# The second graph-attention layer swept head pair by head pair instead of row block by row block

## The reference

```python
xt = jnp.einsum('ni,hio->hno', x, W)              # x: output of layer 0, 4096 x 256
src = jnp.einsum('hnf,hf->hn', xt, a[:, :out_f])
dst = jnp.einsum('hnf,hf->hn', xt, a[:, out_f:])
e = jax.nn.leaky_relu(src[:, :, None] + dst[:, None, :], 0.2)
e = jnp.where(adj > 0, e, -jnp.inf)
h_prime = jnp.einsum('hij,hjf->hif', jax.nn.softmax(e, axis=2), xt)
out = layernorm(x + h_prime.transpose(1, 0, 2).reshape(n, 256))
```

## Time and profile before

| | us |
|---|---|
| median of 3 runs | 2619.55 |
| the profiled execution's own time | 2621.43 |
| its span in the trace | 2619.7 |
| start of the second layer's first group (span time) | 2120.48 |
| start of group 1 | 2157.76 |
| start of its last group | 2581.84 |

### The profile page before, as it was taken

The page is one execution under the profiler, slowest core; times in us unless marked ns, Lnnn a source line. Parts: engine busy times, 40 slices in busy tenths (PEclk is TensorE's granted clock), DMA queues, the critical chain, the costliest instruction groups (busy, mean ns, idle before and its releaser), DMA issues.

```text
span 2619.7 us, 62505 instructions
## 1 busy us (share of the span) xinstructions
PE 2579.8 (98%) x25977; PEld 2300.7 (88%) x25977; DVE 2116.3 (81%) x4315; ACT 2121.9 (81%) x3309; POOL 107.0 (4%) x151
## 2 busy tenths in 40 slices
PE   8999999999999999999999999999999989999998
PEld 6678888888888888888888888888888879999998
DVE  5568888888888888877878778788755689999998
ACT  4578888888888888888888888888873578999997
POOL 1220000000000000000000000000002420000000
PEclk9999999999999999999999999999999999999999
DMA  8975424243342433421212111221226665233430
GB/s 275 321 239 131 111 81 118 63 115 98 90 120 68 124 87 84 110 73 48 64 40 54 50 47 44 60 56 35 62 55 198 228 216 189 95 119 105 132 126 20
DMA packets 324116, 285.02 MB, mean 109 GB/s; under 512 B 124661, under 2 KB 268024, under 8 KB 323834
## 3 DMA queue, kind: packets, MB, share of 16 engines
q1 hardware_dynamic: 290570, 264.51, 34.3%
q10 hardware_dynamic: 33264, 16.52, 2.1%
HBM read 195.13 MB, written 57.74 MB: 97 GB/s over the span
## 4 chain that ended last, share of the span: by engine, by line
PE 88%; DVE 6%; ACT 4%; issue 1%; DMA 0%; SPq 0%; DVEq 0%; ACTq 0%
PE l_ps L912 69%; PE l_ps L1002 8%; PE l_ps L884 4%; PE l_ps L932 4%; ACT l_arena L1238 4%; DVE l_arena L1724 2%; DVE l_arena L1723 2%; PE l_ps L951 1%; DVE l_arena L1749 1%; DVE l_arena L1747 0%; PE l_ps L896 0%; DVE l_arena L1782 0%; DVE l_arena L1712 0%; PE l_ps L857 0%; PE l_ps L943 0%
## 5 line engine op out<-in xcount | busy, mean ns | idle before, releaser
L912 PE MATMUL l_ps<-l_arena 128*128 128x258 f16 x16384 | 1802.4, 273 | 0.6 <-ACT l_arena L1112 0.6
L912 PEld LDWEIGHTS l_ps<-l_arena 128*128 128x128 fp8e4 x16384 | 1603.0, 98 | 200.3 <-ACT l_arena L1112 1.2
L1134 ACT ACTIVATE l_arena<-l_arena 128x512 fp8e4<-128x512 f32 x2048 | 1282.1, 709 | 78.2 <-PE l_ps L912 76.4
L1523 DVE SCALAR_TENSOR_TENSOR l_arena<-l_arena,l_mask 128x512 uint32<-128x512 uint32 x512 | 354.0, 691 | 201.6 <-ACT l_arena L1134 199.3
L1002 PE MATMUL l_ps<-l_arena 128*128 128x130 f16 x8000 | 462.8, 221 | 19.1 <-DVE l_arena L1749 15.1
L1238 ACT ACTIVATE l_arena<-l_arena 128x1024 fp8e4<-128x1024 f32 x434 | 457.6, 1136 | 28.5 <-PE l_ps L1002 28.5
L1002 PEld LDWEIGHTS l_ps<-l_arena 128*128 128x128 fp8e4 x8000 | 459.8, 99 | 22.0 <-issue 19.6
L1524 DVE TENSOR_TENSOR l_arena<-l_arena,l_mask 128x512 uint32<-128x512 uint32 x512 | 354.6, 693 | 0.0
L1503 DVE SCALAR_TENSOR_TENSOR l_arena<-l_arena 128x129 f16<-128x129 f32 x960 | 274.4, 349 | 8.4
L1169 ACT COPY l_arena<-l_ps 128x258 f32<-128x258 f32 x256 | 94.6, 369 | 218.9 <-PE l_ps L912 218.9
L1529 DVE SCALAR_TENSOR_TENSOR l_arena<-l_ps,l_arena 128x258 f32<-128x258 f32 x256 | 116.7, 482 | 115.6 <-ACT l_arena L1169 115.6
(11 more groups left out here) (170 smaller groups left out, 1175.3 us busy)
## 6 DMA issues: line engine op xcount, KB each, us to landing
l_arena<-in_adj SPq DMA_DIRECT2D x58, 1024.0 KB, 6.3
l_arena<-uv SPq DMA_DIRECT2D x125, 272.0 KB, 4.8
l_arena<-l_wh SPq DMA_DIRECT2D x120, 256.0 KB, 4.8
l_arena<-l_srow SPq DMA_DIRECT2D x64, 256.0 KB, 3.3
l_arena<-feat SPq DMA_DIRECT2D x32, 512.0 KB, 3.7
feat<-l_arena ACTq DMA_DIRECT2D x63, 256.0 KB, 2.3
l_wh<-l_arena SPq DMA_DIRECT2D x64, 192.0 KB, 6.9
uv<-l_arena SPq DMA_DIRECT2D x8, 1088.0 KB, 5.7
```

Of the source, the lines that this page charges most:

```text
L912: last = nc.tensor.matmul(sums(t, m), pattern(k, m).bitcast(F8)[:, j, t * P:(t + 1) * P], uv[:, slot(v, order[k]) + j, m * WH:m * WH + 2 * ...
L1134: ins = act.activation(pattern(k, 0).bitcast(F8)[:, j, :], s1b[q][:, :], ACT.Relu, bias=kc[:, h, jt:jt + 1], scale=STEEP, saturate=False)
L1523: dve.scalar_tensor_tensor(c, v, ONE8X4, m, ALU.bitwise_xor, ALU.bitwise_and)
```

## The change

The order of the groups becomes two passes: groups 0 to 7 are heads 0 and 1 over blocks 0 to 3, groups 8 to 15 heads 2 and 3 over the same blocks. Both slots keep their head for a whole pass, so `uv2` is loaded once a pass. The first correction of heads 0 and 1 stays where it was. That of heads 2 and 3 is done in groups 2 to 5 in turns 1, 3 and 5, on one chunk at a time in a small buffer, `visitor`: load, multiply, store, wait, load the next. In pass 1 the residual rows are the 128 left columns in `zh`, which SyncE stores back to `x1` and loads again in every second group; in pass 2 the whole rows are in `z` as before, and head 2 is parked in every block. The statistics and the application move to groups 10 to 15, so that block 2's application and the load of block 3's rows fall into the last group.

```diff
-        G2, FIRST, WHOLE = H2 * NB2, H2, CPB - 2
+        G2, PASS, WHOLE = H2 * NB2, 2 * NB2, CPB - 2
+        visitor = at(88768, F16, 2, JC2, W4)
+        zh = at(76416, F32, 4, TPB2, 2 * D2)
...
+        def head2(g):
+            return g // PASS * 2 + g % 2
+
+        def block2(g):
+            return g % PASS // 2
...
-            def store_back(h, c):
-                cols = slice(c * JC2 * W4, (c + 1) * JC2 * W4)
-                sp.wait_ge(s_res, rescaled(h, c))
-                sp.dma_start(uvd[h][:, cols], uv2[:, h % 2, cols]).then_inc(s_back[h], 16)
+            def far_columns(i):
+                c = i % WHOLE
+                return uvd[2 + i // WHOLE][:, c * JC2 * W4:(c + 1) * JC2 * W4]
+
+            def load_far(i):
+                sp.dma_start(visitor.rearrange("p t w -> p (t w)"), far_columns(i)).then_inc(s_in, 16)
+
+            def store_far(i):
+                sp.wait_ge(s_res, 2 * WHOLE + i + 1)
+                sp.dma_start(far_columns(i), visitor.rearrange("p t w -> p (t w)")).then_inc(s_back, 16)
...
+            def load_half(b):
+                sp.dma_start(zh, half_rows(b)).then_inc(s_zl, 16)
+
+            def store_half(b):
+                sp.wait_ge(s_dz, 2 * b + 2)
+                sp.dma_start(half_rows(b), zh).then_inc(s_xs[b], 16)
...
             for g in range(G2):
-                if g > H2 and g % H2 == 1:
-                    b = g // H2 - 1
+                if g in range(2, PASS + 1, 2):
+                    b = g // 2 - 1
+                    store_half(b)
+                    sp.wait_ge(s_xs[b], 16 * (NT // 4 + 1))
+                    if g < PASS:
+                        load_half(b + 1)
+                    else:
+                        for first, last in parts2:
+                            load_z(0, first, last)
+                if g > PASS + 2 and g % 2 == 1:
+                    b = block2(g) - 1
                     for p, (first, last) in enumerate(parts2):
                         sp.wait_ge(s_ap, 3 * b + p + 1)
                         sp.dma_start(tiles(out, b, first, last), z[:, first:last, :]).then_inc(s_o[p], 16)
...
+                if g == 1:
+                    load_far(0)
+                if 2 <= g < 6:
+                    for i in range(3 * (g - 2), 3 * (g - 1)):
+                        store_far(i)
+                        sp.wait_ge(s_back, 16 * (i + 1))
+                        if i + 1 < 2 * WHOLE:
+                            load_far(i + 1)
                 if g < G2 - 2:
                     sp.wait_ge(s_ca2, CPB * (g + 1))
                     sp.wait_ge(s_cd, owned(g, own[-1]))
                     load_row2(g + 2)
-                    if g < FIRST:
-                        sp.wait_ge(s_back[g], 16 * WHOLE)
+                if PASS - 2 <= g < PASS:
                     for k in range(CPB):
                         sp.wait_ge(s_pe2, CPB * g + k + 1)
                         load_uv(g + 2, k)
-                    if g + 1 < FIRST:
-                        for n in range(WHOLE):
-                            store_back(g + 1, n if g % 2 else WHOLE - 1 - n)
...
+            def add_parked(b):
+                dve.wait_ge(s_zl, 16 * NB2 + 48 * (b + 1))
+                dve.tensor_tensor(z[:, :, 2 * D2:3 * D2], z[:, :, 2 * D2:3 * D2], park, ALU.add)
+
+            def rescale_far(i):
+                h, c = 2 + i // WHOLE, i % WHOLE
+                dve.wait_ge(s_in, 16 * (i + 1))
...
-                    if 0 < g < FIRST - 1 and m >= 6:
-                        for n in range(2 * (m - 6), 2 * (m - 5)):
-                            rescale(g + 1, n)
-                    if g >= H2:
-                        b = g // H2 - 1
-                        if g % H2 == 0 and 1 <= m < 5:
+                    if 2 <= g < 6 and m in (1, 3, 5):
+                        rescale_far(3 * (g - 2) + m // 2)
+                    if g > PASS + 1:
+                        b = block2(g) - 1
+                        if g % 2 == 0 and 1 <= m < 5:
                             final_stats(2 * (m - 1), 2 * m, g)
...
-                if 0 < g < FIRST - 1:
-                    for n in range(4, WHOLE):
-                        rescale(g + 1, n)
             base = 2 * NT + 4 * (NB2 - 1)
+            add_parked(NB2 - 1)
```

More of the change, by code:

```diff
@@ L285, in network @@
         s_us, s_res = s.sem("us"), s.sem("res")
-        s_back = [s.sem(f"back{h}") for h in range(H2)]
+        s_in, s_back = s.sem("in"), s.sem("back")
         s_uv2 = [[s.sem(f"uv{q}{k}") for k in range(CPB)] for q in range(2)]
@@ L791, in _ @@
             sp.wait_ge(s_xp, NT)
-            for first, last in parts2:
-                load_z(0, first, last)
+            load_half(0)
             store_rows(CPB - 2)
-            for c in range(WHOLE):
-                store_back(0, c)
             store_rows(CPB - 1)
@@ L981, in sweep2 @@
                     pe.wait_ge(s_bc2, CPB * g + k + 1)
-                    if g < FIRST and order[k] < WHOLE:
+                    if g < 2 and order[k] < WHOLE:
                         pe.wait_ge(s_res, rescaled(g, order[k]))
                     else:
-                        pe.wait_ge(s_uv2[q][k], 16 * (g // 2 + 1))
+                        pe.wait_ge(s_uv2[q][k], 16 * (g // PASS + 1))
                     for t in range(TPB2):
@@ L1746, in drain2 @@
                     ch = Chain(dve, s_e2, 2 * g + t // batch)
[L1747 removed]
+                    ch.link(dve.tensor_tensor(into, sums2(slice(t, t + batch), 1), sc2[:, head2(g), rows:rows + batch].unsqueeze(
                         2).to_broadcast([P, batch, 2 * V1]), ALU.mult))
@@ L1766, in divide2 @@
                 v = part[:, :, 0:D2]
-                quotient = park if h == 0 and b > 0 else v
+                quotient = park if h == 2 else v
                 ch.link(dve.tensor_tensor(quotient, v, inverse.unsqueeze(2).to_broadcast([P, last - first, D2]), ALU.mult))
-                if h == 0 and b > 0:
+                if h == 2:
                     dve.sem_inc(s_dz, 1)
                     return
-                if h == (b > 0):
-                    dve.wait_ge(s_zl, 48 * (b + 1))
-                if h == 1 and b > 0:
-                    dve.tensor_tensor(z[:, :, 0:D2], z[:, :, 0:D2], park, ALU.add)
-                into = z[:, first:last, h * D2:(h + 1) * D2]
-                dve.tensor_tensor(into, into, v, ALU.add).then_inc(s_dz, 1)
+                if h == 0:
+                    dve.wait_ge(s_zl, 16 * (b + 1))
+                elif h == 3:
+                    add_parked(b)
+                into = (zh if h < 2 else z)[:, first:last, h * D2:(h + 1) * D2]
+                dve.tensor_tensor(into, into, v, ALU.add).then_inc(s_dz, 1)
+            def add_parked(b):
[4 more added lines that the diff above has]
+                dve.wait_ge(s_in, 16 * (i + 1))
+                dve.tensor_scalar(visitor[:, :, 0:2 * V1], visitor[:, :, 0:2 * V1], fu.bitcast(F32)[:, c, h:h + 1], None,
+                                  ALU.mult)
+                dve.tensor_scalar(visitor[:, :, VH:VH + 2 * V1], visitor[:, :, VH:VH + 2 * V1],
+                                  fv.bitcast(F32)[:, c, h:h + 1], None, ALU.mult).then_inc(s_res, 1)
             def final_stats(first, last, ready):
```

31 lines of the change are left out of this document (16 added, 15 removed).

## The result

| | median of the runs, us | lowest to highest |
|---|---|---|
| before, on the same chip | 2618.66 (20 runs) | 2612.35 to 2622.27 |
| changed | 2622.89 (20 runs) | 2616.79 to 2627.18 |

The ratio is 1.0017, 95% interval 1.0011 to 1.0023, that is +4.4 us (2.9 to 6.0). The direction was forecast wrong; the time lies inside the range of 2613.5 to 2626.

What follows compares the result with a forecast made beforehand. The prediction took a loop through ScalarE, VectorE and TensorE to set the steady 29.74 us group, leaving gains only in groups 1 to 3. Terms of -4.88, 0, 0 and +3.4 gave -1.5 us: 2618.0 us, range 2613.5 to 2626.

Steps and rivals of the forecast that it cites:

- What bounds the kernel: Second layer: steady groups, 29.74 us, offer nothing; a group starts at earliest 11.40 us after the comparison; gains only in groups 1 to 3.
- Term 1: Groups 1 to 3: corrections of heads 2 and 3 leave, gaining 1.20, 2.05 and 1.63 us (the last from the clock), 4.88 together.
- Term 2: Groups 2 to 5: visiting chunks cost nothing, as a 4.8 us round trip fits VectorE's 5.2 us of other work.
- rival A: Groups 2 to 5: visitors don't keep up and VectorE waits; 5.2 us at a 6.5 us round trip, time 2623.2; chance 0.16.
- Term 3: Division and statistics: three blocks' statistics still cost 0.12 us each and only move to groups 10, 12, 14; nothing.
- Term 4: Last group: late load of residual rows delays the tail's first reading to +26.35 us, a loss of 3.4 us.
- The sum: Whole kernel: -4.88 + 3.4 = -1.5 us, put on the median 2619.55, gives 2618.0 us.
- C: Last group: the tail is cheaper because the load lands sooner; -3.1 us, time 2616.5; chance 0.09.
- D: Start of the layer, groups 0 and 1, runs better without slot traffic; -6 us, time 2613.6; chance 0.08.
- B: Groups 1 to 3: gain doesn't come, as the slow clock turns up elsewhere; +1.4 us, time 2621; chance 0.12.

Runs made afterwards that it cites:

- e2: The kernel before without the corrections of heads 2 and 3 and their stores back (computation left out); ratio 0.9980, -5.2 us.
- e8: The kernel before, its group order kept, with the corrections of heads 2 and 3 moved to earlier turns, none at a group's end; 2614.58 us, ratio 0.9982.
- e9: No computation, only a 272 KB chunk stored and loaded back 96 times with nothing else on the core; 458.9 us, 4.78 a round trip.
- e4: The changed kernel with two visitor buffers instead of one, loads two corrections ahead; ratio 1.0000 against before.
- e5: The changed kernel, unchanged, timed and traced a second time; ratio 1.0025 against before.
- e7: The changed kernel with two visitor buffers, block 2's early application in the last group, and the parked addition moved from VectorE to GpSimd; ratio 0.9996.
- e6: The changed kernel with block 2's application wholly in turn 1 of the last group, so the last load goes out sooner; ratio 1.0015.
- e1: The kernel before, unchanged, timed and traced a second time; ratio 1.0004 against itself.
- e11: No computation, the 96 store-and-load round trips beside busy VectorE and ScalarE only; 457.4 us, run once.
- e3: The changed kernel with head 3's visiting chunks corrected ahead of head 2's; 2618.43 us, one run.

## Why the prediction was wrong, by its own steps

**What bounds the kernel: right.** Steady groups stayed at 29.74, and 11.40 us from the comparison on was indeed the earliest start: e2 and e8 reach it in groups 2 and 3 and nothing goes below.

**Term 1 (-4.88): right.** e2 -5.2, e8 -4.7. All three parts are there in the traces, group 3's clock too. Group 1 of the changed kernel shows 31.37 at a mean clock of 0.95; that slow start was there before and is no gain or loss of the change.

**Term 2 (0): the step that failed first.** It read: the wait is nothing, by 0.4 us, since the round trip is 4.8 us by the undisturbed rows. The two rows were each true, and e9 confirms them 96 times, but nothing in groups 2 to 5 keeps a store undisturbed: TensorE's fetches go on. Its stores took 2.0 to 4.5 us, the round trip up to 7.2. The price over the steady pace was 2.9 us in one trace and 5.2 in the other; taking the mechanism away (e4) moved the ratio from 1.0017 and 1.0025 to 1.0000. This is rival A in the size the prediction gave for 6.5 us (5.2 us), at the chance of 0.16. Its own formula fits: a store of 4.2 and a load of 2.7 make 6.9, 1.7 over the 5.2 of the turns, and VectorE waited 1.78; 3.4 and 2.7 make 6.1, 0.9 over, and it waited 0.96. Part of that agreement is luck: rival A has all four groups late, the traces have one or two, and 1.6 of the 5.2 us in e5 are the clock. I had put the excess of the medians of the earlier trace rows down to the slot traffic and taken the row without any, though the spare time was only 0.4 us. For many of those stores that was so: four issued 0.5 us behind one another from 2189.70 on took 3.3 to 3.9 us without a fetch. But the trace of before also had the other kind: of two stores issued 3.5 us apart, the one at 2175.20 landed in 2.0 us, the one at 2178.66, which a fetch met 0.45 us behind its issue, in 3.5. The formula of the Trainium skill that stands beside the term (2.0 us plus the bytes at 436 GB/s, 2.6 us either way) is given in that section for transfers issued from GpSimd; these are issued from SyncE, and alone they took 2.0 and 2.7 us (e9). It would have missed the wait as well.

Term 2 also missed the clock's part: one wait of 2.62 us was followed by a stretch at half clock and 1.6 us more (e5), the very loss that term 1 took away from group 3.

**Term 3 (0): wrong by 1.8 us.** It counted the statistics as 0.12 us a block "as before; they only move". What had to be counted was what stands next to them: in pass 2 the parked addition, 0.6 us, is directly ahead of each statistics group, and VectorE has no pause left there (it is busy for 30.11 of the 30.46 us). 30.46 - 29.86 = 0.6, three times. e7 took the addition away and had 29.85.

**Term 4 (+3.4): right in mechanism, 0.5 too large.** The last group is 2.9 us longer (40.76 against 37.86), the first reading at +25.83 and released by the load. The store went out at 2598.09 (+20.05, forecast +20.06) and landed in 2.1 us; the load behind it took 3.0 us where its row had 3.5, and that is the half microsecond. e6 shows the rest: the load 1.2, the split behind the application 1.7, where 1.8 was forecast. The forecast that a fall of the clock in the closing would stay covered was nearly borne out: e5 has the fall, and a last group 0.3 us longer.

**The sum.** -4.9 (term 1) + 2.9 to 5.2 (term 2) + 1.8 (term 3) + 2.9 (term 4) = +2.7 to +5.0 us; the runs say +4.4 (2.9 to 6.0). With e4's second buffer it is -0.2, measured 0.0 (-2.4 to +2.1). Rivals C and D didn't come: the tail was cheaper by 0.5 us only, and the slow start of the layer stayed (groups 0 and 1 take 36.68 and 31.37 us in the changed kernel's first trace, 37.47 and 32.21 in e5; 36.41 for group 0 in e1, the kernel before). B's lost gain didn't come either, but its sign, a low clock that turns up in another group, did: in group 4 of e5 and group 5 of e6, behind the waits that the visitors cause.

## What to carry to other kernels

A chain of dependent transfers over one buffer needs spare time against a slow landing, not against the fastest one in the trace; here a landing could be 2.5 us later than the fastest, the spare time was 0.4, and a second buffer took the whole wait away (e4). When work is moved between groups, write down what it will stand next to: two loads that each fitted into a pause don't fit into the same one. Before restructuring loops to take work off the end of a group, try to move that work a few turns earlier: that had the whole gain here (e8) and none of the costs. A late transfer whose packets come in two parts is worth a look at the instruction queue.

## What the runs showed of the hardware that I had not expected

- A 272 KB store from on-chip memory lands in 2.0 to 2.3 us on an idle core, 96 times of 96, and in up to 4.7 us when a 16 KB instruction fetch of TensorE falls into it: a sixteenth of its rows then starts when the fetch's packet ends. A load of 2.7 us became one of 3.05 to 3.9 in the same case. Busy VectorE and ScalarE alone did nothing (e11); with TensorE the 96 round trips took 485.3 us instead of 477.2, one run each.
- The clock fell to its lower level (1.2 GHz) after some idle times of TensorE and not after others. In the ten traces of the full kernel (before, changed, e1 to e8), second layer from group 1 on, it never fell behind the nine idle times of 1.65 to 2.08 us. Of seven between 2.12 and 2.25 us, four were followed by a fall (2.12 and 2.13 ahead of group 3 before, in both traces; 2.24 ahead of the closing in e3 and e5) and three not (2.13 ahead of group 6 in e5; 2.25 ahead of the closing in the changed kernel's first trace and in e4). Behind 2.33 (e6), 2.62 (e5) and the 4.1 ahead of group 1 (ten times) the slow matmuls were always there. (The 2.25 ahead of group 0 stands behind other matmuls and is left aside.) So near 2.2 us the length of the idle time does not settle it. Each fall behind an idle time of 2.1 to 2.6 us cost TensorE 1.6 us on top of it.
- An addition of 128x512 on GpSimd went with a slowing of VectorE's split from 1.2 to 2.30 us, and itself took 1.27 us in one group and 2.0 to 3.5 in the others.
